# Causal mask of the transposed scores: from mask products on TensorE to selects on GpSimd

## What is computed

```python
Q = _rope(split_heads(x @ W_q.T), pos)
K = _rope(split_heads(x @ W_k.T), pos)
score = jnp.einsum('bnqd,bnkd->bnqk', Q, K) / jnp.sqrt(jnp.float32(D_K))
causal = jnp.triu(jnp.ones((s, s), dtype=bool), k=1)
score = jnp.where(causal[None, None], -jnp.inf, score)
attn = jax.nn.softmax(score, axis=-1)
out = jnp.einsum('bnqk,bnkd->bnqd', attn, V)
```

## Time and profile before

| | us |
|---|---|
| median of three runs | 965.01 |
| lowest and highest run | 961.19, 965.33 |
| the profiled execution | 970.2 |
| its span in the profile | 968.0 |
| share of the span: PE (TensorE) | 84% |
| DVE (VectorE) | 66% |
| ACT (ScalarE) | 46% |
| POOL (GpSimd) | 44% |

### The profile page before, as it was taken

The page is one execution under the profiler, slowest core; times in us unless marked ns, Lnnn a source line. Parts: engine busy times, 40 slices in busy tenths (PEclk is TensorE's granted clock), DMA queues, the critical chain, the costliest instruction groups (busy, mean ns, idle before and its releaser), DMA issues.

```text
span 968.0 us, 19930 instructions
## 1 busy us (share of the span) xinstructions
PE 811.1 (84%) x6324; PEld 597.3 (62%) x6324; DVE 641.1 (66%) x1850; ACT 449.8 (46%) x731; POOL 423.0 (44%) x408
## 2 busy tenths in 40 slices
PE   3559887887988997897978987989998999888755
PEld 2427464564664764664745555868886888777622
DVE  5686857689688788788687664644643334977616
ACT  2205544645654654654644656545554555444300
POOL 3132213116516427427314335476677655655421
PEclk9758989999998898998997879899999999989878
DMA  4586845335537437436496213554566758888582
GB/s 175 131 206 169 241 92 132 88 88 149 152 99 171 141 98 191 130 85 192 131 334 189 92 49 108 159 182 145 162 213 215 208 163 315 315 289 305 209 348 97
DMA packets 88147, 168.40 MB, mean 174 GB/s; under 512 B 14192, under 2 KB 55664, under 8 KB 87792
## 3 DMA queue, kind: packets, MB, share of 16 engines
q1 hardware_dynamic: 74224, 128.59, 46.0%
q0 software_dynamic: 13824, 38.55, 10.5%
HBM read 90.15 MB, written 76.68 MB: 172 GB/s over the span
## 4 chain that ended last, share of the span: by engine, by line
PE 30%; DVE 9%; DMA 7%; issue 4%; POOL 3%; SPq 3%; ACT 2%; DVEq 0%; POOLq 0%; ACTq 0%
PE ring L1540 9%; PE ring L1561 4%; DMA xg<-sorted_rows 3%; PE ring L1526 2%; DVE nmax L833 2%; POOL expert_rows L736 2%; PE ring L1440 2%; PE ring L1318 2%; PE ring L1320 2%; PE ring L1319 2%; PE ring L1396 2%; DMA q_st<-mrow 2%; DMA expert_rows<-ys,dest 1%; SPq L628 1%; PE ring L1332 1%
## 5 line engine op out<-in xcount | busy, mean ns | idle before, releaser
L736 POOL DMA_INDIRECT expert_rows<-ys,dest x160 | 159.0, 994 | 94.3 <-ACT ys L1199 44.5
L1248 ACT ACTIVATE prob<-ring 128x1024 f32<-128x1024 f32 x128 | 130.1, 1022 | 144.7 <-PE ring L1387 144.3
L833 DVE TENSOR_REDUCE nmax<-ring 128x2 f32<-128x768 f32 (+1 forms) x192 | 158.2, 862 | 26.3 <-PE ring L1369 25.1
L728 POOL DMA_INDIRECT sorted_rows<-xr,idx_all x128 | 126.6, 989 | 96.7 <-DVE xr L995 63.4
L1540 PE MATMUL ring<-we,xh 128*128 x640 | 158.9, 393 | 0.0
L1540 PEld LDWEIGHTS ring<-we,xh 128*128 128x128 f32 x640 | 120.7, 199 | 14.2
L1058 DVE SCALAR_TENSOR_TENSOR sl<-sl,got,ring 128x128 f32<-128x128 f32 x160 | 48.3, 343 | 104.2 <-ACT sl L1300 104.1
L1396 PE MATMUL ring<-prob,v_sb 128*32 128x512 f32 (+3 forms) x1024 | 97.3, 479 | 3.3 <-ACT prob L1248 3.3
L1362 PE MATMUL ring<-k_st,q_st 48*128 48x384 f32 (+3 forms) x512 | 80.4, 374 | 20.9 <-DVE nmax L830 10.3
L706 POOL TENSOR_TENSOR rot<-rot 128x512 f32<-128x512 f32 x14 | 17.9, 1276 | 160.0 <-DVE rot L810 160.0
L1381 PE MATMUL ring<-maskt_b,halves_b 64*128 64x128 bf16 (+2 forms) x640 | 50.7, 238 | 42.2 <-DMA q_st<-mrow 20.7
(11 more groups left out here) (205 smaller groups left out, 1687.7 us busy)
## 6 DMA issues: line engine op xcount, KB each, us to landing
xg<-sorted_rows SPq DMA_DIRECT2D x160, 134.0 KB
parts<-part SPq DMA_DIRECT2D x32, 512.0 KB, 5.8
ykt<-expert_rows SPq DMA_DIRECT2D x14, 1024.0 KB, 10.0
k_st<-parts SPq DMA_DIRECT2D x64, 128.0 KB
q_st<-parts SPq DMA_DIRECT2D x64, 128.0 KB
we<-w_exp SPq DMA_DIRECT2D x1, 6144.0 KB, 21.4
sorted_rows<-zeros SPq DMA_DIRECT2D x2, 2144.0 KB, 9.0
sorted_rows<-zeros SPq DMA_DIRECT2D x32, 134.0 KB
```

What stands on the lines that cost most here:

```text
L728: pool.indirect_dma_start(out=xs[group_of(s)], out_offset=bass.IndirectOffsetOnAxis(ap=idx_all[:, s, t, k:k + 1], axis=0), in_=xr[:, s % 2 ...
L736: pool.indirect_dma_start(out=yk, out_offset=bass.IndirectOffsetOnAxis(ap=dest[:, j % 8, b:b + 1], axis=0), in_=ys[:, j % NYS, b, :], in_o ...
L833: dve.tensor_reduce(nmax[:, Q % 2, :, pp, qb], slot[:, :, col:col + (qb + 1) * P], AX.X, ALU.max, negate=True).then_inc(s_max, 1)
L1248: act_e.activation(prob[:, u % 2, 2 * half:2 * half + 2, :], slot[:, :, :], ACT.Exp, scale=SCALE).then_inc(s_exp, 1)
```

## The change

GpSimd writes zeros into the diagonal blocks of the exponentials, in place, after ScalarE wrote them: one `affine_select` for each key block of a value unit, over 128 partitions and four heads of 128 columns (it keeps an element where the query's column is at least the key's partition, and writes 0 elsewhere). That is one for unit 0, two for unit 1 and one for unit 2. GpSimd does this at the plan's place of the unit's last transposed piece. The value unit waits for the selects (`s_causal`) in place of the exponentials. The four mask products of each transposed piece go, and with them the table `maskt_b` and its column block among the constants. The mask of the first scores stays.

```diff
+            def mask_weights(Q, m):
+                u = UNITS * Q + m
+                pool.wait_ge(s_exp, ST_DONE[Q, V_AFTER[m]])
+                for kb, col in V_PARTS[m]:
+                    diagonal = prob[:, u % 2, :, col:col + P]
+                    pool.affine_select(diagonal, diagonal, pattern=[[0, 4], [1, P]], compare_op=ALU.is_ge, fill=0.0,
+                                       base=0, channel_multiplier=-1).then_inc(s_causal, 1)
...
+                elif kind == "ST" and st[2] in V_AFTER:
+                    mask_weights(n, V_AFTER.index(st[2]))
...
             def transposed_unit(Q, m, slot):
 
-                parts = ST_PARTS[m]
-                diagonal = [col // P for half, kb, col in parts]
-                for h in range(2):
-                    for par in range(2):
-                        r = slice(64 * par, 64 * par + 64)
-                        mask = maskt_b[r, h, 0:64 * (h + 1)].unsqueeze(1).to_broadcast([64, len(parts), 64 * (h + 1)])
-                        pe.matmul(blocks_of(slot[:, par, :], diagonal)[:, :, 0:64 * (h + 1)], halves_b[r, h, :], mask,
-                                  start=h == 0, stop=False, skip_group_check=True)
-                for half, kb, col in parts:
+                for n, (half, kb, col) in enumerate(ST_PARTS[m]):
                     k0, width = kb * P, T - kb * P
                     for par in range(2):
                         r = slice(64 * par, 64 * par + MROWS)
                         last = pe.matmul(slot[:, par, col:col + width], k_st[r, Q % NQ, half, k0:k0 + P],
-                                         q_st[r, Q % NQ, half, k0:T], start=False, stop=True, skip_group_check=True)
+                                         q_st[r, Q % NQ, half, k0:T], start=n == 0, stop=True, skip_group_check=True)
                 last.then_inc(s_ST, 1)
...
                 elif kind == "AV":
                     m = st[2]
-                    pe.wait_ge(s_exp, ST_DONE[n, V_AFTER[m]])
+                    pe.wait_ge(s_causal, NT * n + sum(len(parts) for parts in V_PARTS[:m + 1]))
```

More of the change, by code:

```diff
@@ L30 @@
 C_ALL = C_GATE + KD * E
-K_IDENT, K_HALVES, K_MASK, K_MASKT, K_BELOW = 0, P, 3 * P, 5 * P, 7 * P
-K_TIE = 8 * P
+K_IDENT, K_HALVES, K_MASK, K_BELOW = 0, P, 3 * P, 5 * P
+K_TIE = 6 * P
 K_BIAS = K_TIE + NG * NG
@@ L299, in block_kernel @@
         mask_b = place("mask_b", [P, 2, P], bf16)
-        maskt_b = place("maskt_b", [P, 2, P], bf16)
         below_b = place("below_b", [P, P], bf16)
@@ L425, in block_kernel @@
         s_exp = sem("exponentials")
+        s_causal = sem("exponentials_masked")
         s_av = sem("pv_step")
@@ L661, in _ @@
             sp.dma_start(stage[:, C_O:], w_small[:, C_O:]).then_inc(s_small, 16)
-            sp.wait_ge(s_init, 8)
+            sp.wait_ge(s_init, 7)
             for st in PLAN:
@@ L749, in _ @@
             pool.memset(v_sb[:, :, :, :, DH:DH + 1], 1.0).then_inc(s_vone, 1)
-            pool.wait_ge(s_init, 8)
+            pool.wait_ge(s_init, 7)
             for st in PLAN:
@@ L1110, in _ @@
             dve.wait_ge(s_const, 16)
-            for made, col in ((halves_b, K_HALVES), (mask_b, K_MASK), (maskt_b, K_MASKT)):
+            for made, col in ((halves_b, K_HALVES), (mask_b, K_MASK)):
                 dve.tensor_copy(made[:, :, :].rearrange("p h c -> p (h c)"), kc[:, col:col + 2 * P]).then_inc(s_init, 1)
@@ L1442, in sum_results @@
                 last.then_inc(s_cp, 1)
-            pe.wait_ge(s_init, 8)
+            pe.wait_ge(s_init, 7)
             for st in PLAN:
@@ L1609, in constant_table @@
         np.where(c2 % P > half, MASKED, 0.0),
-        np.where(half > c2 % P, MASKED, 0.0),
         p < c,
```

## The result

The changed kernel took 1002.49 us (median of four runs, 995.82 to 1006.94), the kernel before 963.1 us beside it. The ratio is 1.040 with a 95% interval of 1.0356 to 1.0443: 39 us slower. 1011 us were forecast, in a range of 968 to 1055.

What follows compares the result with a forecast made beforehand. TensorE was taken to set the pace in attention, busy 87%. 69 us late - 17 absorbed - 9 products + 3 clock = +46 us, on 965 us, gave 1011 us; range 968 to 1055 us.

Steps and rivals of the forecast that it cites:

- What bounds the kernel: In attention (72 to 600 us) TensorE sets the pace, busy 87%; GpSimd, busy 37%, has room by the average.
- The mask products, -9 us: On TensorE in attention, removing four products from each of 160 units saves 10 us of work, 9 us of time.
- goes by TensorE's share in attention: Step turning 10 us of removed TensorE products into time gained: 10 x 0.87 = 9 us.
- The select, 1.1 us: On GpSimd, each of 128 selects of 128x512 float32 takes 1.1 us, taken nearer to a two-operand tensor_tensor; outer bound 2.0.
- the prediction's own signs: Profile signs of error: selects near 0.6 or over 1.6 us (price), value products hardly waiting (slack), loss behind 600 us (place).
- The lateness, 69 us: At the 96 value units in attention, value products start late behind GpSimd's selects, 69 us in all.
- cheap rival: Selects on GpSimd cost only the write, 0.62 us: 36 us late, +10 us in sum, 975 us; chance 0.15.
- same layout: Selects placed in GpSimd's order over recorded times, their ends compared with value products' recorded starts; 69 us late at 1.1 us each.
- What is absorbed, 17 us: In attention, a quarter of TensorE's 68 us idle, 17 us, takes up lateness; ends none and 45 us.
- The clock, +3 us: In attention, new waits bring one more fall of TensorE's granted clock, 3 us; range 0 to 15.

Runs made afterwards that it cites:

- kernel without mask: Kernel before with the transposed scores' mask left out altogether: no mask products, no selects, value products waiting for exponentials; 966.5 us, ratio 1.003.
- apart run: Changed kernel, but GpSimd's second low part (a_lo of unit 1) waits until VectorE has done the sequence's first three routing steps; 1002.1 us.
- unlinked run: Changed kernel with the selects working on a spare tile and the value products waiting for the exponentials alone; 995.6 us.
- write-only run: Unlinked run with a memset of the same 512 elements on the spare tile in place of each select; 985.8 us.

## Why the prediction was right, and where it was not

The direction, the range and the size came out (39 us against 46), and the size by luck: two wrong terms nearly cancel. The forecast has 52 us more idle (69 late less 17 absorbed) and 3 us of clock; the profiles show 14.7 and 32.9. Step by step:

- **What bounds the kernel.** Right: the loss is in attention, which grew by 35 us while the whole span grew by 32.6, and GpSimd's average share (37% before, 274.17 / 563.7 = 49% after) said nothing of it.
- **The mask products, -9 us.** The cost was right as work (-10.4 us), and wrong as time: 0, by two pairs of kernels (963.3 to 966.5 and 953.2 to 954.1). The step that failed is "goes by TensorE's share in attention". It left out that a TensorE with less to do was granted less clock.
- **The select, 1.1 us.** 0.642 us, a factor of 1.7 too dear. I took the row of a tensor_tensor with two operands as nearest; the memset's line (0.62 us) was the better guide, if partly by chance, for a memset of 512 elements itself took 0.53. By the prediction's own signs, selects near 0.6 us mean that the price was wrong. The Trainium skill, "GPSIMD Engine Reference", section 4.1 (Engine selection), puts one-input operations at roughly line rate; the select's 0.64 us beside the memset's 0.53 agrees.
- **The lateness, 69 us.** At the cheap rival's 0.62 us the same layout gives 36 us; at 0.64 the value products waited 37.7. The method held, and the pattern too: 25.3 us of the waits are at unit 1, 6.2 each at units 0 and 2.
- **But the cheap select's rival gave +10 us.** With its price and its 36 us true, the kernel lost 39; my own sum at that price is 36 - 17 - 9 + 3 = 13 us. So the layout was not what set the time. Cutting the link returned only 7 us.
- **What is absorbed, 17 us.** From waits of 34 us more to idle of 14.7 more, 20 us were absorbed: right in size. Yet the idle that is left has another cause than the value products, since it is 82.6 us without the link too. VectorE, which I had read as bound in this stretch, was stretched by 23.5 us, and that I had not costed at all: I never asked what the new instruction does to the durations of its neighbours.
- **The clock, +3 us.** +32.9 us (27 by the estimate above), outside my range for it (0 to 15) and as large an error as the lateness, the other way. I had taken one fall for the whole kernel. Attention has 22 stretches at half clock in place of 13, 184 us of them in place of 106. The kernel without mask has 13 of 130 us in all: as many, and longer.

By time, the loss is a ladder of kernels that differ in one thing each: before 963.3, no mask 966.5, GpSimd's waits in its order +7.1, an instruction of 0.53 us at each +12.2, a select in its place +9.8, the link +6.9, changed 1002.5. Each rung has its share of clock, so the ladder and the split are two views of the same 39 us and are not added. In the splits the rung of 12.2 us is surcharge (+12.7, idle +0.8), the next mostly idle (+8.4, surcharge +1.2), and the link surcharge again (+8.3, idle 0). Open are how much of the +9.8 is reading and how much length; how much of the two rungs' 22 us comes through VectorE's stretched instructions, for no run shortens these alone and gains time; and at which rows exactly the granted clock of the thinner kernels fell: the split shows that it did in both pairs, but not by what rule.

## What to carry to other kernels

Where VectorE is nearly full, an instruction moved to GpSimd is not free because GpSimd has room: look which VectorE instructions run beside it, what they read and write, and what it pushes along in GpSimd's queue. Where TensorE's granted clock moves between its levels, cost a removal or a wait in work, idle and surcharge, for work taken away can return as surcharge. And a stretch in which TensorE waits for 1 to 2 us again and again may be worth filling with products of zeros: 92 of them made the kernel before 1.3% faster, where taking 640 mask products away made nothing faster.

## What the runs showed of the hardware that was not expected

- A VectorE sum of 64 elements with both inputs in SBUF took 1.72 us instead of 0.22 when GpSimd's subtraction of 512 elements ran beside it, and ended with it; GpSimd's was recorded as starting 0.34 us later than VectorE's. A scatter on GpSimd was under way when the sum started; in the apart run, beside the same scatter and without the subtraction, the sum took 0.23 us. It also kept 0.22 us in the kernel before beside an rstd of four elements.
- Scalings of 256 elements from SBUF to SBUF (xr and pr) took 0.55 to 0.59 us on average instead of 0.42 and 0.47, in the kernels with selects and with memsets of 512 elements alike; the longest xr took 0.84 us in the unlinked run and 0.77 in the write-only run; two-input steps of 16 elements stretched in the kernel with selects (350 and 279 ns) and not in that with memsets (167 and 175).
- An in-place select of 512 float32 elements on GpSimd takes 0.642 us, one of four elements 0.199; a memset of 512 takes 0.532, of four 0.106.
- With products of zeros in front of its waits, TensorE was granted 1.00 in a stretch of 55 us that had 0.88 without them, and 0.96 instead of 0.92 over attention.
